# GpSimd's pauses reckoned at their measured pace and kept to the end, idle products in TensorE's planned waits, groups of 4, 4 and 8 units, and x loaded by two queues

## The reference, cut to what matters

```
x = x + 0.5 * moe(layernorm(x))                      # first expert layer
x = x + rnn(layernorm(x))                            # recurrence
x = x + 0.5 * moe(layernorm(x))                      # second expert layer, same weights
moe(x): e = argmax(x @ router_w.T) of each token; y = square(relu(x @ fc[e])) @ proj[e]   # 8 experts, 128 -> 512 -> 128
rnn(x): h[t] = tanh(x[t] @ Wi.T + bi + h[t-1] @ Wh.T + bh)   # 512 steps, one after the other
```

## Time and profile before

| | |
|---|---|
| runs | 600.45, 600.04, 594.44 us; median 600.04 |
| the profiled execution | 603.88 us, span 602.0 us, mean granted clock 0.98 |
| busy | TensorE 551.4 us (92%), its weight loads 533.7, VectorE 412.8 (69%), ScalarE 315.4 (52%), GpSimd 423.5 (70%) |
| of TensorE's: L1687 and L1677 | 198.3 and 193.2 us, 1248 passes each |
| of TensorE's: steps L1697 | 158.0 us, 1024 passes |
| of GpSimd's: pauses L1152 | 116.0 us, 187 of them, 620 ns each |
| of GpSimd's: indirect DMAs | 263 of about 985 ns |
| the chain of waits that ended last | TensorE 74%, VectorE 11%, no visible cause ("issue") 7%, DMA 2% |

### The profile page before, as it was taken

How to read it: one execution, slowest core, us unless ns; L and a number is a source line. 1 busy time by engine, 2 the same in 40 slices (tenths; PEclk the granted TensorE clock), 3 DMA queues, 4 the chain that set the end, 5 groups by cost and what they waited for, 6 DMA issues and landing times.

```text
span 602.0 us, 16237 instructions
## 1 busy us (share of the span) xinstructions
PE 551.4 (92%) x4714; PEld 533.7 (89%) x4714; DVE 412.8 (69%) x1507; ACT 315.4 (52%) x1089; POOL 423.5 (70%) x520
## 2 busy tenths in 40 slices
PE   7799798997999989999999999998999999869991
PEld 6798698897999989999999999997889999658991
DVE  5789867886667878657876774577546466665661
ACT  2133165464666546666666666654346666425660
POOL 2699497789995778978874987838849638664552
PEclk9889999998999999999999999999999999998997
DMA  5977432221222223322321532101152301435310
GB/s 184 296 273 289 109 105 81 79 78 59 78 80 69 66 82 97 93 68 63 98 81 49 132 111 77 39 27 68 45 144 76 84 20 69 139 115 151 101 37 1
DMA packets 54163, 58.89 MB, mean 98 GB/s; under 512 B 8999, under 2 KB 42034, under 8 KB 54080
## 3 DMA queue, kind: packets, MB, share of 16 engines
q1 hardware_dynamic: 44064, 36.68, 21.0%
q0 software_dynamic: 9440, 21.06, 10.8%
q10 hardware_dynamic: 576, 0.13, 0.1%
HBM read 27.67 MB, written 30.62 MB: 97 GB/s over the span
## 4 chain that ended last, share of the span: by engine, by line
PE 74%; DVE 11%; issue 7%; DMA 2%; SPq 1%; ACT 1%; another core or an unknown queue 1%; ACTq 0%; POOLq 0%; DVEq 0%
PE yp L1687 23%; PE hp L1677 20%; PE z L1697 11%; PE mT L1583 4%; PE lg L1627 3%; PE xTp L1666 3%; PE hp L1702 3%; DMA hsT<-in_L_attn_x_dram 2%; PE z L1647 2%; PE yp L1707 2%; DVE pay L1238 2%; DVE r_sb L1361 2%; PE hp L1616 1%; SPq L1012 1%
## 5 line engine op out<-in xcount | busy, mean ns | idle before, releaser
L1687 PE MATMUL yp<-projT,s_sb 128*128 x1248 | 198.3, 291 | 11.6 <-ACT s_sb L1495 5.9
L1677 PE MATMUL hp<-xT_sb,w_sb 128*128 128x128 f32 x1248 | 193.2, 286 | 2.0 <-DVE xT_sb L1355 1.3
L1687 PEld LDWEIGHTS yp<-projT,s_sb 128*128 128x128 f32 x1248 | 161.3, 194 | 14.6 <-issue 14.2
L1466 ACT ACTIVATE hsT<-z 128x16 f32<-128x16 f32 x512 | 93.5, 183 | 147.5 <-PE z L1697 102.7
L1677 PEld LDWEIGHTS hp<-xT_sb,w_sb 128*128 128x128 f32 x1248 | 161.7, 193 | 3.1 <-DVE xT_sb L1355 1.4
L1697 PEld LDWEIGHTS z<-hsT,wT 128*128 128x128 f32 x1024 | 154.0, 190 | 8.9 <-ACT hsT L1466 3.0
L1697 PE MATMUL z<-hsT,wT 128*128 128x16 f32 x1024 | 158.0, 230 | 1.4 <-ACT hsT L1466 1.2
L1495 ACT ACTIVATE s_sb<-r_sb 128x256 f32<-128x256 f32 (+1 forms) x252 | 115.7, 461 | 74.5 <-issue 51.8
L1361 DVE TENSOR_SCALAR r_sb<-hp 128x512 f32<-128x512 f32 x156 | 106.9, 686 | 66.6 <-PE hp L1677 55.9
L1152 POOL MEMSET idle<- 128x600 f32 x187 | 116.0, 620 | 0.2
L1189 POOL DMA_INDIRECT out_dram<-y_sb,xs_sb x71 | 70.1, 988 | 61.7 <-DVE y_sb L1368 34.9
(11 more groups left out here) (132 smaller groups left out, 564.3 us busy)
## 6 DMA issues: line engine op xcount, KB each, us to landing
xs_sb<-xs_dram SPq DMA_DIRECT2D x71, 129.0 KB
xs_sb<-xy_dram SPq DMA_DIRECT2D x85, 64.0 KB
xy_dram<-y_sb SPq DMA_DIRECT2D x85, 64.0 KB
xy_dram<-zeros SPq DMA_DIRECT2D x10, 512.0 KB, 6.0
hsT<-in_L_attn_x_dram SPq DMA_DIRECT2D x16, 256.0 KB
hsT<-n_L_ffn_expert_proj_dram SPq DMA_DIRECT2D x2, 1024.0 KB
fc_sb<-in_L_ffn_expert_fc_dram SPq DMA_DIRECT2D x1, 2048.0 KB
out_dram<-y_sb,xs_sb POOLq DMA_INDIRECT x71
```

Source lines behind the costliest of these rows:

```text
L1466: act.activation(state(t), z_step(t), ACT.Tanh).then_inc(s_h, 1)
L1677: mm = pe.matmul(hp[:, g % 2, h * P:(h + 1) * P], w_sb[:, g % 2, h * P:(h + 1) * P], xT_sb[:, g % 2, :], start=True, stop=True)
L1687: mm = pe.matmul(yp[:, 0:D], s_sb[:, g % 2, h, :], projT[:, bass.ds(offsets[g] + h * D, D)], start=(h == 0), stop=(h == HC - 1))
```

## The change

- `FIRST` is 4, 4, 8 units: the tiles of the groups are 23, 23 and 39, still 85. `STEP` stays 1, 3, 1, so in the second group three units are complete after 19 of its tiles and the fourth after 23. `SECOND` is 4, 3, 3, 2, 2, 1, 1 and `MIDDLE` 1 nine times, then 2, 2, 2, 1.
- `REST = 600` becomes `REST, PACE = 0.48, 1.75`: the pause on the chip stays a write of 600 columns; the plan takes 0.48 us for it, 1.75 us for a row (ROW), and drains one DMA in 1.75 us instead of 1.85. The condition `t < T` is gone.
- Until the first tile is chosen, `fill` puts as many idle products as fit (0.25 us each) into each wait that the plan has on TensorE; the one product at the end of each beat is gone. `EARLY` is 8 instead of 4.
- Units 1 and 3 of x are issued by ScalarE, ahead of Wi and Wh. `AHEAD` is 2, 4, 7: two units of x between the first zeros and proj, two between proj and fc, none after.
- In the plan the estimate of a norm is 1.4 instead of 1.1 us and that of a unit of x 1.3 instead of 1.1; the settings `PR` are others.

```diff
-FIRST = [5, 3, 8]
+FIRST = [4, 4, 8]
 STEP = [1, 3, 1]
-MIDDLE = [1, 1, 1, 1, 1, 1, 1, 1, 1, 1, 3, 3]
-SECOND = [3, 2, 2, 3, 2, 2, 1, 1]
+MIDDLE = [1, 1, 1, 1, 1, 1, 1, 1, 1, 2, 2, 2, 1]
+SECOND = [4, 3, 3, 2, 2, 1, 1]
...
-REST = 600
+REST, PACE = 0.48, 1.75
...
-PR = {'proj': -38.387, 'lat1': 30.338, 'lat2': 69.811, 'lat3': -18.484, 'last': 24.985,
-      'hor': 76.814, 'beat': 7.803, 'put': -37.848, 'dve': 2.211, 'act': 2.454, 'pe': 2.181,
-      'early': 0.245, 'load': 3.526, 'hold': -32.825, 'slack': 198.928, 'near': 0.015,
-      'tol': -0.155, 'mix': -6.094, 'late': 4.266, 'root': 80.638, 'gather': -76.836,
-      'scatter1': 17.849, 'scatter2': 77.955, 'crit': 18.203, 'front': 3.982, 'dvx': 1.459,
+PR = {'proj': -24.384, 'lat1': 38.464, 'lat2': 16.638, 'lat3': -13.853, 'last': 29.433,
+      'hor': 107.488, 'beat': 7.703, 'put': -24.921, 'dve': 2.201, 'act': 2.708, 'pe': 2.163,
+      'early': 0.283, 'load': 3.662, 'hold': -24.24, 'slack': 112.715, 'near': 0.036,
+      'tol': 0.127, 'mix': -7.274, 'late': 0.379, 'root': 80.609, 'gather': -101.48,
+      'scatter1': -8.609, 'scatter2': 11.874, 'crit': 18.133, 'front': 5.404, 'dvx': 1.683,
       'burst': 0.3}
-EARLY, WARM = 4, 1
-AHEAD = [4, 5, 7]
+EARLY = 8
+AHEAD = [2, 4, 7]
...
-            at += {"rows": 1.1, "proj": 4.0, "fc": 8.0}[what[0]]
+            at += {"rows": 1.3, "proj": 4.0, "fc": 8.0}[what[0]]
...
-    ROW, LAND, WINDOW = 1.27 + REST / 900, 2.2, 3.413
+    ROW, LAND, WINDOW = PACE if REST else 1.35, 2.2, 3.413
...
         if what in ("norm", "mnorm"):
-            return 1.1
+            return 1.4
...
-                while REST and t < T and drained > start + PR["burst"]:
+                while REST and drained > start + PR["burst"]:
                     pool_order.insert(-1, ("rest",))
-                    start += REST / 900
-                pool_free, drained = start + 1.27, max(drained, start) + 1.85
+                    start += REST
+                pool_free, drained = start + 1.27, max(drained, start) + PACE
...
+            def fill(place):
+
+                n = int((need[0] - pe) / 0.25) if not order else 0
+                if n > 0:
+                    b.idle[place] = n
+                    matmuls(2 * n, 128, 0.0)
+
             def passes(place, n, columns, keys, result=None):
                 yield from here(place, *keys)
                 yield keys
+                fill(place)
                 at = matmuls(n, columns, need[0])
...
-            for _ in range(b.warm):
-                matmuls(2, 128, 0.0)
...
+        def by_act(u):
+
+            return u < FIRST[0] and u % 2 == 1
+
...
                 if what[0] == "rows":
-                    rows_in(what[1])
+                    if not by_act(what[1]):
+                        rows_in(what[1])
...
         @block.scalar
         def _(act):
+            for u in range(min(FIRST[0], NU // 2)):
+                if by_act(u):
+                    act.dma_start(raw(u), x[:, u * UNIT:(u + 1) * UNIT, :].rearrange("b (th j) d -> th b (j d)", j=UR)
+                                  ).then_inc(s_in[u], 16)
             act.dma_start(w_raw[:, 0, :], Wi).then_inc(s_w, 16)
...
                 def step_at(place):
                     if place in b.at_place:
                         step(b.at_place[place])
+                    warm_up(b.idle.get(place, 0))
...
-                warm_up(b.warm)
                 for p in b.pe:
                     if p[0] == "rank":
+                        warm_up(b.idle.get("rank", 0))
                         rank(p[1])
```

More of the change, by code:

```diff
@@ L96, in __init__ @@
         self.pe, self.tail, self.front, self.dve, self.proj = [], [], [], [], []
-        self.warm = 0
+        self.idle = {}
         self.quick, self.by_dve, self.at_place, self.until = False, False, {}, {}
@@ L424, in warm @@
                 matmuls(2, FILL, 0.0)
-            fill = alone and len(b.steps)
+            lone = alone and len(b.steps)
             if after is not None:
@@ L435, in on_pe @@
                 yield from turn("t0", slots[0])
-            elif fill:
+            elif lone:
                 warm()
@@ L444, in on_pe @@
                 yield from split("p%d" % i, p, 0)
-            if fill > 1 and not products:
+            if lone > 1 and not products:
                 warm()
@@ L453, in on_pe @@
                 yield from turn("t1", slots[1])
-            elif fill > 2:
+            elif lone > 2:
                 warm()
@@ L462, in on_pe @@
                 yield from split("q%d" % i, p, 1)
-            if fill > 3 and not products:
+            if lone > 3 and not products:
                 warm()
@@ L469, in on_pe @@
                 yield ("pr", min(2 * p[1] // E, 1)), ("proj", p[1] - 2) if p[1] >= 2 else ("weights",)
+                fill("proj%d" % p[1])
                 ev["tr", p] = matmuls(4, 128, need[0])
-            for _ in range(b.warm):
-                matmuls(2, 128, 0.0)
             for p in b.pe:
@@ L475, in on_pe @@
                     yield ("pick", p[1]), None
+                    fill("rank")
                     ev[p] = matmuls(p[1].J // 2 + 1, 64, need[0])
@@ L744, in plan @@
         jobs = [j for j in jobs if j[1]]
-        b.warm = int(not order and WARM)
         play(b, behind, after)
@@ L878, in build @@
         warm = sb("warm", [P, 1])
-        idle = sb("idle", [P, max(REST, 1)])
+        idle = sb("idle", [P, 600])
         stats = sb("stats", [P, 2, 4, 6])
@@ L1151, in rest @@
                     pool.wait_ge(s_idle, rests[0])
+                else:
+                    pool.wait_ge(s_blank, 2)
                 pool.memset(idle[:, :], 0.0).then_inc(s_idle, 1)
@@ L1780, in _ @@
                 for p in b.proj:
+                    warm_up(b.idle.get("proj%d" % p[1], 0))
                     turn_proj(p[1])
-                warm_up(b.warm)
                 for p in b.pe:
                     if p[0] == "rank":
+                        warm_up(b.idle.get("rank", 0))
                         rank(p[1])
```

## The result

| | before | after |
|---|---|---|
| median of the runs, us | 600.25 (594.44 to 604.12) | 578.32 (574.89 to 579.49) |
| ratio | | 0.966, 95% interval 0.957 to 0.974 |
| the profiled execution, its span | 603.88, 602.0 | 578.79, 576.4 |

The kernel before took 602 to 612 us (medians) on the other chips of the experiments, so these are compared by ratio, or within one chip. Some executions are disturbed and run some per cent longer; ratios leave them out, and two kernels that mostly ran so have none.

The account below looks back on a forecast made before the run. It took GpSimd's work ahead of unit 3's gathers, with the 24.5 us pause after state 95, as the bound. Terms -2, -6, -7, -1 and +1 gave -15: 589 for the profiled execution, 585 as median, range 568 to 605.

Parts of the forecast that it names:

- GpSimd's start: Head: with four units instead of five in the first group, the first scatter goes out 2 us earlier (1 to 5).
- GpSimd's waits: GpSimd ahead of unit 3's gathers: half of its waits of 7.62, 0.95 and 3.05 us go, -6 us.
- rival A: Unit 3's gathers go ahead of the third group's scatters, the recurrence runs without a pause: 568 us, chance 0.11.
- The late add: Unit 3's add, 13.2 us behind its last gather, comes earlier once the plan has GpSimd's true pace: -7 us.
- Unit 4 "is covered": State 128: unit 4's gathers follow unit 3's by 7 us while 32 steps take 23, so no pause there.
- The first tile at 55 to 60: TensorE's first product starts at 55 to 60 us instead of 69.87; priced at 0 because GpSimd sets the pause.
- The idle products keep clock 1.0: Head: the new fill keeps TensorE's granted clock at 1.0, from 24 to 35 us; worth 0.
- The pauses at the end: After state 511: pauses between GpSimd's last DMAs delay the last scatter, costing 0 to 3.6 us, taken as +1.
- 0.72 us a step afterwards: Recurrence after the pause: each step still takes 0.72 us; slower than 0.74 would make TensorE the bound.
- The end, 83 to 90 us: Stretch after state 511: 83 to 90 us, where the kernel before took 85.4.
- Rival C: Third group's scatters ahead of unit 1's gathers, stop at state 31: 611 us, chance 0.16; smaller case: only unit 2 delayed.
- case B: Nothing to measure: GpSimd's waits and unit 3's late add stay, 598 to 602 us; chance 0.19.

Follow-up runs that it names:

- a1_warm: The kernel after with one more idle product in every TensorE beat without work ahead of the first tile: 578.65 us.
- b3_unit3: The kernel before with unit 3's gathers put ahead of most of the third group's scatters: 612.76 beside 612.12 us, ratio 0.998.
- a2_norm11: The kernel after with the plan's estimate of a norm put back from 1.4 to 1.1 us: 612.8 us, ratio 1.000.
- b4_groups: The kernel before with the change's FIRST, MIDDLE and SECOND lists alone: 629.01 beside 610.25 us, ratio 1.030.
- a11_450: The kernel after with GpSimd's pauses as writes of 450 columns instead of 600: 574.72 us, ratio 0.961.
- b7_unit3_end: The kernel before with unit 3's gathers put ahead and GpSimd's pauses kept to the end: 602.77 beside 601.6 us, ratio 1.000.
- a7_tT: The kernel after with the condition `t < T` back, so GpSimd pauses only while states are left: 588.73 us, ratio 0.963.
- b6_end: The kernel before with the condition `t < T` taken out, so GpSimd pauses to the end: 609.81 us, no ratio.
- a6_onequeue: The kernel after with all units of x loaded by SyncE: 580.98 us.
- a9_ahead: The kernel after with the old AHEAD, 4, 5, 7 in place of 2, 4, 7: 598.6 us, ratio 0.982.
- a10_norest: The kernel after with all 229 of GpSimd's pauses left out: 806.49 us, ratio 1.322.

## Why the prediction came out

The number held: 585, range 568 to 605, and 578.3 measured, faster. The sum of terms did not: it had -15 for a profiled execution that lost 25.1, nearly all from unit 3's gathers and add in an order that would stay as it was. The order did not stay, and terms that the sum had at nothing or with the other sign carried the time. That they came out inside the range is luck in good part. By its steps:

- **GpSimd's start, -2: failed.** The last unit's statistics are at 12.12 instead of 13.93, the 1.8 us sooner that I took, but the first scatter goes out at 24.13, before 24.07. It waits 7.29 us for the positions, and these begin with `pick` at 17.91, before at 17.33. There `pick` waited for the last logits; now the first norms stand ahead of it in VectorE's order and wait 3.51 us for the root. TensorE is at the 1.2 GHz level in 10 to 24 us, where it was at 2.4 GHz before, but its last logits end at 17.72, ahead of `pick`; a1_warm, at 0.63 there, gains only 0.2 us.
- **GpSimd's waits, -6: failed, and the step's premise with it.** The waits of 7.62, 0.95 and 3.05 us are now 3.53, 3.43 and 5.10: the sum is 12.1 instead of 11.6. And I had the third group's scatters stay ahead of unit 3's gathers. They changed places, which is rival A's mechanism, and unit 3's gathers came 53.5 us sooner. b3_unit3 shows that this order alone removes the pause, and a2_norm11 that a norm estimate decides the order; I had compared the plan's urgencies as if both pieces were ready, and not asked when the norms are.
- **The late add, -7, by the pace: the gap shrank about as much, the cause isn't shown.** Unit 3's add stands 7.1 us behind its last gather instead of 13.2, and unit 4's, which now follows the 32 scatters, 2.6 us. With the old pace it is 15.8 us for unit 3 in b4_groups. But in b3_unit3, with the old pace too, unit 3's add stands 13.1 us behind its last gather (132.48) with no long run of rows ahead of it, and unit 4's, directly behind the run, only 7.3. The cause stays open.
- **Unit 4 "is covered": failed.** Its gathers follow the 32 scatters, not unit 3, and wait for the stores of its tiles, which set their time: with the scatters out 3.2 us sooner they go 0.4 us sooner (a11_450). The pause of 8.3 us is theirs. Rival A had no such pause, so A failed there too.
- **The first tile at 55 to 60: right,** 59.44. Priced at 0 because GpSimd was in the way; it no longer is. What it brings can't be separated from the rest: b7_unit3_end, without it, reaches state 128 14.8 us later.
- **The idle products keep clock 1.0: in the stretch that I named, not in the head.** In 24 to 35 us it is 0.97 instead of 0.53, but in 10 to 24 us 0.52 instead of 1.00, and 0.50 to 0.61 in 45 to 72. Their worth of 0 was right (a1_warm).
- **The pauses at the end, +1 (0 to +3.6): wrong in sign.** They shorten the end by 11.0 us in the kernel after (a7_tT), by 10.3 in b3_unit3 (b7_unit3_end) and by about 1 in the kernel before (b6_end). I had counted only GpSimd's own delay, and that was right: its last scatter stands 21.7 us behind the last state, before 21.5. What the scatters do to the others, did not show by itself.
- **0.72 us a step afterwards: nearly.** 280.2 / 384 = 0.730, before 275.6 / 384 = 0.718; TensorE is busy for 374.9 of the 379.3 us between first and last state.
- **The end, 83 to 90 us:** 80.0.

Rival C's smaller case, "if only unit 2 is swallowed ... that is case B again", happened in a2_norm11: unit 2 begins at 197.0, and the time is that of the kernel before.

What is shown: that the order makes and removes the pause, that the pauses at the end shorten it, and which settings cost when they are taken back. Parts put into the kernel before gave nothing (b3_unit3, b7_unit3_end) or cost 3% (b4_groups). Of single parts taken from the kernel after, the queue costs nothing clear of noise (a6_onequeue), the pauses at the end 11 us of the end (a7_tT), `AHEAD` some 20 us (a9_ahead, 595.0 to 602.8 beside 572.4 to 583.0) and the norm's estimate the whole gain (a2_norm11). So the gain is not a sum over parts; that it belongs to one plan in which they fit is my reading. How much of it the earlier first tile carries was not measured alone, and neither `PACE` nor the factors `PR` were tried alone.

## What to carry over

A pause of the critical recurrence during which the busiest engine works isn't lost until that engine runs dry, so set up that engine's account (real work, idle, idle products) between fixed marks before pricing the pause. When a plan decides the order, ask for every competing piece when it becomes ready, not only which is more urgent; 0.3 us in one estimate was worth 34 us (612.8 beside a1_warm's 578.65). And a pause on an engine may be there for what its neighbours suffer: price taking it out and putting it in by their rows.

## What the runs showed of the chip

Beside GpSimd's indirect DMAs of 128 rows, issued 1.26 us apart, TensorE, VectorE and ScalarE stop together, 17 times for 1.7 to 8.7 us (a10_norest); in the longest of these stops the DMA engines are 16% busy. At 1.50 us apart there are no such stops of over 1.5 us, and the kernel still loses 80 us or more (658 and up beside 578); at 1.62 us it loses nothing. In a7_tT a stop of 4.0 us began behind four DMAs issued 1.26 to 1.27 us apart, with the DMA engines 66% busy in 498 to 500 us. The kernel before issues its last DMAs at 1.27 us too, and there only single engines wait with no releaser, 1.1 to 3.6 us; so the distance alone doesn't decide. What the engines wait for, the trace doesn't name.
